# A pre-normed layer of differential attention and a zoned feed-forward: Wb's weighting on ScalarE, lambda's chain ahead of feed-forward, X summed on TensorE

## What is computed

```python
xn = layernorm(x)                                  # without weights
out = x + attention(xn) + feed_forward(xn)

# attention: 16 half heads of 8 features for q and k, 8 heads of 16 for v
q, k, v = xn @ Wq.T, xn @ Wk.T, xn @ Wv.T          # q, k with rotary tables
probs = softmax(q @ k.T)                           # per half head
lam = exp(sum(lq1 * lk1)) - exp(sum(lq2 * lk2)) + LAMBDA_INIT
attn = (probs[even] - lam * probs[odd]) @ v
attn = attn * rsqrt(mean(attn**2) + 1e-5) * (1 - LAMBDA_INIT)
attention = attn @ Wo.T

# feed_forward: a router picks 3 of 8 zones per sequence, with weights w
z = sum over the 3 zones e of w[e] * (gelu(xn @ Wa[e]) @ Wb[e])
feed_forward = xn + z
```

## Time and profile before

| | |
|---|---|
| three runs | 435.41, 437.92, 437.03 us; median 437.03 |
| profiled execution | 436.09 us, its span 433.6 us |
| PE busy | 414.3 us (96%) |
| DVE busy | 384.8 us (89%) |
| ACT busy | 338.5 us (78%) |
| POOL busy | 141.3 us (33%) |
| feed-forward's second halves | from 39.6 us |
| attention's exponentials | from 141.5 us to 418.3 |
| TensorE's granted clock, mean | 0.992 |

### The profile page before, as it was taken

How to read it: one execution, slowest core, us unless ns; L and a number is a source line. 1 busy time by engine, 2 the same in 40 slices (tenths; PEclk the granted TensorE clock), 3 DMA queues, 4 the chain that set the end, 5 groups by cost and what they waited for, 6 DMA issues and landing times.

```text
span 433.6 us, 7697 instructions
## 1 busy us (share of the span) xinstructions
PE 414.3 (96%) x2742; PEld 191.7 (44%) x2742; DVE 384.8 (89%) x743; ACT 338.5 (78%) x450; POOL 141.3 (33%) x172
## 2 busy tenths in 40 slices
PE   8899999999999999999999999999999999999983
PEld 6665556666655333333333333333333333345442
DVE  4995999999998899999999999999999998888476
ACT  3786656655553799899899989989999999889971
POOL 4269999878763500111020110120112201000002
PEclk9999999999998999999999999999999999999998
DMA  9736751400000070020002064000000000000003
GB/s 269 295 87 221 235 210 51 139 9 1 3 0 2 2 245 1 3 97 3 2 2 99 1 130 68 3 2 2 2 4 0 3 0 3 3 2 2 2 2 97
DMA packets 21871, 24.94 MB, mean 58 GB/s; under 512 B 11818, under 2 KB 16106, under 8 KB 21578
## 3 DMA queue, kind: packets, MB, share of 16 engines
q1 hardware_dynamic: 21096, 23.60, 17.8%
q10 hardware_dynamic: 738, 0.86, 0.8%
HBM read 14.49 MB, written 8.65 MB: 53 GB/s over the span
## 4 chain that ended last, share of the span: by engine, by line
PE 71%; DVE 14%; ACT 7%; issue 5%; DMA 1%; POOL 1%; ACTq 0%; POOLq 0%; DVEq 0%
PE ps L1399 21%; PE ps L1362 16%; PE ps L1252 13%; DVE part_max L905 7%; ACT E L795 5%; PE ps L1324 4%; PE ps L1177 3%; PE ps L1179 3%; PE ps L1178 3%; PE ps L1325 2%; PE ps L1326 2%; PE ps L1390 2%; DMA X<-in_x 1%; PE ps L1380 1%; DVE stats L859 1%
## 5 line engine op out<-in xcount | busy, mean ns | idle before, releaser
L905 DVE TENSOR_REDUCE part_max<-ps 128x1 f32<-128x512 f32 x512 | 320.2, 680 | 26.6 <-PE ps L1252 22.4
L795 ACT ACTIVATE E<-ps 128x1024 f32<-128x1024 f32 x256 | 245.3, 1029 | 30.6 <-PE ps L1362 27.2
L1399 PE MATMUL ps<-E,Vg 128*32 128x512 f32 x896 | 119.3, 605 | 0.0
L1252 PE MATMUL ps<-K,Q 32*128 32x512 f32 x384 | 106.9, 466 | 1.1 <-DVE part_max L905 0.4
L1362 PE MATMUL ps<-Q,K 32*128 32x512 f32 x320 | 70.7, 489 | 2.1 <-ACT E L795 1.4
L1362 PEld LDWEIGHTS ps<-Q,K 32*128 32x128 f32 x320 | 28.6, 181 | 82.7 <-ACT E L795 72.3
L559 POOL TENSOR_TENSOR hL<-h,hH 128x512 fp32r<-128x512 f32 x48 | 61.3, 1286 | 11.6 <-ACT hH L763 11.3
L1252 PEld LDWEIGHTS ps<-K,Q 32*128 32x128 f32 x384 | 45.7, 183 | 24.8 <-DVE part_max L905 18.6
L761 ACT ACTIVATE h<-ps 128x512 f32<-128x512 f32 x48 | 28.8, 599 | 32.1 <-PE ps L1179 22.6
L610 POOL TENSOR_TENSOR U<-AT,rsum 128x256 f32<-128x256 f32 x15 | 9.3, 621 | 104.3 <-DVE rsum L1057 104.3
L1252 PE MATMUL ps<-xnL,xnH 32*128 32x512 f32 x128 | 41.9, 453 | 0.9 <-DVE part_max L905 0.7
(11 more groups left out here) (166 smaller groups left out, 405.1 us busy)
## 6 DMA issues: line engine op xcount, KB each, us to landing
K<-k_scr SPq DMA_DIRECT2D x5, 512.0 KB, 3.8
Q<-q_scr SPq DMA_DIRECT2D x5, 512.0 KB, 7.1
tab<-in_tables SPq DMA_DIRECT2D x2, 1024.0 KB, 10.0
wa_raw<-in_wa SPq DMA_DIRECT2D x6, 256.0 KB, 2.7
wb_raw<-in_wb SPq DMA_DIRECT2D x6, 256.0 KB, 2.9
Q<-max_turned SPq DMA_DIRECT2D x80, 2.0 KB
X<-in_x SPq DMA_DIRECT2D x2, 512.0 KB, 7.0
k_scr<-V SPq DMA_DIRECT2D x2, 512.0 KB, 10.9
```

The lines of the kernel that those rows point to most:

```text
L795: nc.scalar.activation(E[:, par, 2 * jj:2 * jj + 2, :].rearrange("p j t -> p (j t)"), ps[:, 2 * jj:2 * jj + 2, :].rearrange("p j t -> p (j ...
L905: nc.vector.tensor_reduce(part_max[:, tile // FC % 2, j * FC + tile % FC, sh:sh + 1], ps[:, SLOT_BANK[x], :], AX.X, ALU.max).then_inc(slot ...
L1252: mm(ps[:, SLOT_BANK[x], :], Qs[g % KQ_BUFS][strip(j), tile % TB * P:(tile % TB + 1) * P], Ks[g % KQ_BUFS][strip(j), sh * BANK:(sh + 1) * ...
L1399: last = mm(ps[QUAD * j:QUAD * (j + 1), B_PV, :], Vg[:, par, st, j // 2, :], E[:, s % 2, k, :], start=(st == 0), stop=(st == TB - 1), skip ...
```

## The change

Three things are changed, on all five queues.

- *Weighting.* `wb_zone` moves from DVE to ACT, where it is two activations with the zone's weight as scale, both from the raw Wb: one into wb_f, one into the high part. It stands behind gelu of a zone's unit 4. POOL's low part waits for both, SP's `raw_next` for the second.
- *Lambda.* The three parts become one, ahead of the loop of units.
- *The end.* In steps 101 to 113 POOL splits X into two fp32r parts, which take the place of xn's parts in xnH and xnL (groups 3 and 4 of K and Q lay there, their scores are done), and makes an identity in fp32r. At the end PE multiplies both parts by the identity into the product's bank, and Wo's product is added on top. So the additions on POOL and DVE are gone, and ACT copies all four banks to the output rows. `shares_ahead` covers two chunks instead of three, chunk 2 goes the way of chunk 3 with its own root on ACT, and DVE's order at the end is another.

```diff
-LAMBDA_AT = (30, 34, 38)
-
-AHEAD = CHUNKS - 1
+AHEAD = CB
+
+X_SPLIT_AT = (101, 105, 109, 113)
...
                 sp.wait_ge(wa_split, e + 1)
                 sp.sem_inc(sp_waited, 1)
-                sp.wait_ge(wb_done, e + 1)
+                sp.wait_ge(wbh_done, e + 1)
                 raw_load(e + 2, zones[e + 2])
...
             for c in range(CHUNKS):
-                if c < CB:
-                    sp.wait_ge(added, c + 1)
-                else:
-                    sp.wait_ge(o_added, c - CB + 1)
+                sp.wait_ge(o_done, c + 1)
...
+            def x_parts(c):
+
+                t = slice(c * BANK, (c + 1) * BANK)
+                if c == 0:
+                    pool.wait_ge(x_done, TILES + CHUNKS)
+                    pool.sem_inc(pool_waited, 1)
+                    pool.wait_ge(st_done[0], 2 * STEPS * KQ_BUFS)
+                    pool.sem_inc(pool_waited, 1)
+                    pool.wait_ge(st_done[1], 2 * STEPS * KQ_BUFS)
+                    nc.gpsimd.tensor_copy(identR[:], ident).then_inc(id_done, 1)
+                nc.gpsimd.tensor_copy(xnH[:, t], chunk_rows(X, c)).then_inc(x_high, 1)
+                pool.wait_ge(x_high, c + 1)
+                nc.gpsimd.tensor_tensor(xnL[:, t], chunk_rows(X, c), xnH[:, t], ALU.subtract).then_inc(x_split, 1)
...
-            def wb_zone_high(e):
-                act.wait_ge(wb_done, e + 1)
-                nc.scalar.activation(wbH[:, e % 2, :], wb_f[:, e % 2, :], ACT.Copy).then_inc(wbh_done, 1)
+            def wb_zone(e):
+
+                par = e % 2
+                act.wait_ge(raw_in[par], 32 * (e // 2 + 1))
+                if e == 0:
+                    act.wait_ge(wbc_done, 1)
+                if e >= 2:
+                    act.wait_ge(hs_free, H_BUFS + UZ * (e - 1))
+                w = wbc[:, e:e + 1]
+                nc.scalar.activation(wb_f[:, par, :], wb_raw[:, par, :], ACT.Identity, scale=w).then_inc(wb_done, 1)
+                nc.scalar.activation(wbH[:, par, :], wb_raw[:, par, :], ACT.Identity, scale=w).then_inc(wbh_done, 1)
...
-                if n % UZ == 5 and n // UZ + 1 < PICKS:
-                    wb_zone_high(n // UZ + 1)
+                if n % UZ == 4 and n // UZ + 1 < PICKS:
+                    wb_zone(n // UZ + 1)
...
-            squares(CHUNKS - 1)
-            for c in range(CB):
+            def product_copy(c):
                 act.wait_ge(o_ps, c + 1)
                 nc.scalar.activation(chunk_rows(RES, c), ps[:, O_BANK[c], :], ACT.Copy).then_inc(o_done, 1)
+
+            roots(AHEAD)
+            squares(CHUNKS - 1)
+            product_copy(0)
             roots(CHUNKS - 1)
+            for c in range(1, CHUNKS):
+                product_copy(c)
...
-                if n % UZ == 2 and n // UZ + 1 < PICKS:
-                    wb_zone(n // UZ + 1)
-                if n in LAMBDA_AT:
-                    lambdas(LAMBDA_AT.index(n))
...
             square_sums(0)
             square_sums(1)
+            quarter_rows(0)
+            shares_ahead()
             square_sums(2)
-            shares_ahead()
-            quarter_rows(0)
             normalise(0)
             turn_rows(0)
             normalise(1)
+            turn_rows(1)
             quarter_rows(1)
-            turn_rows(1)
+            shares(2)
             normalise(2)
+            square_sums(3)
             turn_rows(2)
-            square_sums(3)
             shares(3)
             normalise(3)
             turn_rows(3)
...
+            def residual(c):
+                if c == 0:
+                    pe.wait_ge(id_done, 1)
+                t = slice(c * BANK, (c + 1) * BANK)
+                pe.wait_ge(x_split, c + 1)
+                mm(ps[:, O_BANK[c], :], identR[:], xnH[:, t], start=True, stop=False, skip_group_check=True)
+                mm(ps[:, O_BANK[c], :], identR[:], xnL[:, t], start=False, stop=False, skip_group_check=True)
...
             pe.wait_ge(exp_done, 2 * ALL_STEPS)
             heads_sum(3, range(GB - 1))
+            residual(0)
+            residual(1)
+            heads_sum(3, (GB - 1,))
             product(0)
-            heads_sum(3, (GB - 1,))
             product(1)
+            residual(2)
             product(2)
+            pe.wait_ge(a_out, 2 * GROUPS + 1)
+            residual(3)
             product(3)
```

More of the change, by code:

```diff
@@ L227, in build @@
             ("X", [P, TILES, P], F32), ("cst", [P, C_END], F32), ("wo_in", [P, P], F32),
-            ("grow", [P, TILES], F32), ("XN", [P, TILES, P], F32),
+            ("grow", [P, TILES], F32), ("identR", [P, P], F32R), ("XN", [P, TILES, P], F32),
             ("V", [P, GROUPS * TB * 2 * QUAD], F32),
@@ L300, in build @@
         grow_done, x_done = sem("grow_done"), sem("x_done")
-        zb_done, z_in, added = sem("zb_done"), sem("z_in"), sem("added")
+        zb_done, z_in, id_done, x_high, x_split = (
+            sem("zb_done"), sem("z_in"), sem("id_done"), sem("x_high"), sem("x_split"))
         wh_done, w_split = sem("wh_done"), sem("w_split")
@@ L327, in build @@
             sem("at_done"), sem("rsum_done"), sem("u_free"))
-        heads_ps, sq_done, ss_done, std_done, rcp_done, rms_done, an_done, ant_done, o_ps, o_done, o_added = (
+        heads_ps, sq_done, ss_done, std_done, rcp_done, rms_done, an_done, ant_done, o_ps, o_done = (
             sem("heads_ps"), sem("sq_done"), sem("ss_done"), sem("std_done"), sem("rcp_done"), sem("rms_done"),
-            sem("an_done"), sem("ant_done"), sem("o_ps"), sem("o_done"), sem("o_added"))
+            sem("an_done"), sem("ant_done"), sem("o_ps"), sem("o_done"))
         u_last = sem("u_last")
@@ L528, in wb_zone_low @@
                 par = e % 2
+                pool.wait_ge(wb_done, e + 1)
+                pool.sem_inc(pool_waited, 1)
                 pool.wait_ge(wbh_done, e + 1)
@@ L641, in _ @@
                     sums_add(SUMS_ADD_AT.index(s))
+                if s in X_SPLIT_AT:
+                    x_parts(X_SPLIT_AT.index(s))
                 if s % TB == 3 and s > TB:
                     shares_of_rows(s // TB - 1)
[L645 to L653, removed]
         @block.scalar
@@ L772, in sums_copy @@
                 nc.scalar.activation(zT[:, c * BANK:(c + 1) * BANK], ps[:, c, :], ACT.Copy).then_inc(z_out, 1)
-            wb_zone_high(0)
+            wb_zone(0)
             strip_evacuate(2)
@@ L956, in _ @@
             xn_low(3)
[L958 to L964, removed]
             dve.wait_ge(logit_ps, 1)
@@ L1010, in _ @@
             rotary(4)
-            wb_zone(0)
             reduce_slot(0, 2)
@@ L1014, in _, with lambdas @@
             rotary(5)
-            def lambdas(part):
+            def lambdas():
                 nl, ab, cc, c2, nlc = (lt[:, k:k + 1] for k in range(5))
[L1018 to L1035, removed]
@@ new lines, in lambdas @@
+                dve.wait_ge(lam_exp, 1)
+                link(nc.vector.scalar_tensor_tensor(nl, lam_e[:, 1:2], LAMBDA_INIT, lam_e[:, 0:1],
+                                                    ALU.subtract, ALU.subtract))
+                link(nc.vector.tensor_scalar(ab, nl, -1.0, None, ALU.mult))
+                link(nc.vector.tensor_tensor(ab, ab, nl, ALU.max))
+                link(nc.vector.tensor_scalar(ab, ab, 1.0, None, ALU.add))
+                link(nc.vector.reciprocal(cc, ab))
+                link(nc.vector.tensor_scalar(cc, cc, LAMBDA_RANGE, 1.0, ALU.mult, ALU.min))
@@ new lines, in lambdas @@
+                link(nc.vector.tensor_tensor(c2, cc, cc, ALU.mult))
+                link(nc.vector.tensor_scalar(epsc[:], c2, EPS, SQRT_LEAST, ALU.mult, ALU.max))
+                link(nc.vector.tensor_scalar(limit[:], c2, FLT_MAX, None, ALU.mult))
+                link(nc.vector.tensor_tensor(nlc, nl, cc, ALU.mult))
+                link(nc.vector.tensor_scalar(comb[:], cst[:, C_E0:C_E0 + 2 * QUAD], cc, None, ALU.mult))
+                nc.vector.scalar_tensor_tensor(comb[:], cst[:, C_E1:C_E1 + 2 * QUAD], nlc, comb[:],
+                                               ALU.mult, ALU.add).then_inc(comb_done, 1)
@@ L1037, in _ @@
+            lambdas()
             for n in range(UNITS):
@@ L1102, in shares @@
             def shares(c):
-                dve.wait_ge(std_done, 1)
+                dve.wait_ge(std_done, c - AHEAD + 1)
                 nc.vector.reciprocal(sd[:, c, :], sd[:, c, :]).then_inc(rcp_done, 1)
-                dve.wait_ge(rcp_done, 1)
+                dve.wait_ge(rcp_done, c - AHEAD + 1)
                 nc.vector.scalar_tensor_tensor(sd[:, c, :], ss[:, c, :], limit[:, 0:1], sd[:, c, :],
                                                ALU.is_le, ALU.mult).then_inc(rms_done, 1)
-                dve.wait_ge(rms_done, 2)
+                dve.wait_ge(rms_done, c - AHEAD + 2)
             def normalise(c):
@@ L1147, in _ @@
             turn_rows(3)
-            def residual(c):
-                dve.wait_ge(x_done, TILES + CHUNKS)
-                dve.wait_ge(o_ps, c + 1)
```

(5 more changed lines are left out.)

3 lines of the change are left out of this document (2 added, 1 removed).

## The result

The changed kernel takes 430.57 us in the median of four runs (429.37 to 431.15), the kernel before 436.22 (435.19 to 437.92). The ratio is 0.9883, 95% interval 0.9858 to 0.9909: 5.1 us faster, between 4.0 and 6.2. The forecast was 431.4, 5.5 faster. So the size came out; of the five parts one was off by 0.9 us, and another, the end, by 0.3 the other way.

The account below looks back on a forecast made before the run. It took POOL and PE, with DVE nearly full, to bound feed-forward, and PE and DVE attention. Terms 3.0 + 0 + 0 + 0 + 2.5 = 5.5 us gave 431.4 us, range 429.0 to 434.2.

Parts of the forecast that it names:

- part 3: Start of feed-forward: lambda's twelve operations ahead of the units fit DVE's idle time; 0 us, bounds 0 and +1.
- part 5: End of the kernel: new DVE order and X's additions gone from POOL and DVE; 2.5 us gained, bounds 1.0 and 3.2.
- three for "right": Trace signs named beforehand as confirming, on unit intervals and starts, DVE's return, its idle time and the end's 1.15 us operation.
- the held operation: DVE operation at the end, 1.15 us, said to wait for POOL's additions and fall to 0.3 without them.
- sign for "wrong": Trace signs named beforehand as refuting: PE waiting behind a weighting or before the last product, lambda's operations over 1 us, longer steps.
- Part 1: Feed-forward: Wb's weighting leaves DVE, so PE's late units come back; 3.0 us gained, bounds 1.5 and 3.9.
- zone 1's 0.86: Feed-forward: delay of the interval behind zone 1's weighting, said to be swallowed by full POOL but for about 0.2 us.
- Part 2: Feed-forward: ACT's two activations per zone, 0.63 us each, make the next gelu some 0.35 late but cost nothing.
- the pinned chain of part 1: Feed-forward, early units: POOL's low part, then ACT's gelu, then PE's product; full POOL keeps PE from coming earlier.
- The slower rival: Start: all twelve lambda operations wait out a POOL operation, DVE 10 us late, 441 us; chance 0.03.
- Part 4: Attention steps 101 to 113: X's four copies and four subtractions on mostly idle POOL, about 7.6 us of work, cost 0.
- if that dip goes: Rival: TensorE's clock dip between 120 and 140 us vanishes, up to 1.8 us less; chance 0.12 together with a second dip.

Follow-up runs that it names:

- lam_late: The changed kernel with lambda's twelve operations moved into attention, one a step in steps 60 to 71; ratio to the kernel before 0.9883.
- wb_only: The kernel before with only the weighting of Wb moved to ACT, lambda and the end as before; ratio 0.9982.
- x_only: The kernel before with X in two parts on PE and ACT's copies, but DVE's old order at the end; ratio 0.9995.
- order_only: The kernel before with DVE's new order, shares ahead for two chunks and chunk 2's own root, additions of X as before; ratio 0.9950.
- lam_only: The kernel before with only lambda's twelve operations put in one piece ahead of feed-forward; ratio 0.9973.
- tail_only: The changed kernel with the weighting back on DVE and lambda back in the units, so the changed end alone; ratio to the kernel before 0.9924.
- one_wah: The changed kernel with four of lambda's two-tensor operations reading a scalar operand, and Wa's high parts for zones 1 to 5 on ACT; ratio to before 0.9853.
- changed again: The changed kernel unaltered, run again beside other variants on the same chip; ratio to the kernel before 0.9871.

## Why the prediction was right, and where not

The forecast time was right, and in part by luck: part 3 was 0.9 us too good and part 5 0.3 too bad, so the sum of 5.5 stands beside 4.9 us in the traces' stages. Of the signs that it named, three for "right" came (intervals from unit 12 on at 2.02, no DVE idle before the third square sum, the held operation at 0.25), and three did not: unit 8 was 0.75 later and not unmoved, unit 45 2.0 earlier and not 3, DVE back at 41.66 and not at 39.7. One sign for "wrong" came as well, lambda's operations over 1 us.

**Part 1, the weighting: right.** The sum of 3.0 us was made for a start without loss. lam_late, which has such a start, is 2.95 ahead of before at unit 45. The claim that POOL swallows zone 1's 0.86 but for 0.2 was the risky one; wb_only gives 0.14.

**Part 2, ACT: right.** Each activation takes 0.72, not 0.63. The gelu behind a pair is 0.2 late (77.72, where PE's products had ended at 77.51), and no interval of PE shows it.

**Part 3, lambda in front: this step failed.** The prediction took 0, with bounds 0 and +1, because "the pinned chain of part 1 takes such a delay up without loss by unit 8". DVE's delay itself was in the text (five operations, back at 40 to 41; it was 41.66, 1.92 late). Two things were wrong. Nearly all of it reached PE, 1.75 us at unit 1: the ring gives PE four slots, and it needed two reductions more to issue the six in front of unit 1's second half. And a pin takes up a delay only as far as PE had been ahead of it. By part 1's own sum PE would have been 0.86 ahead; the rest of 1.75, 0.9, stays, near the upper bound. It is there: 17.92 at unit 8 for 17.01 in lam_late, which lacks the delay, 92.76 at unit 45 for 91.83; and the two intervals in which the pin holds PE in lam_late (2.36 and 2.50, units 6 to 8) are 2.02 in the changed kernel. I counted the same 0.86 twice, once as given up to POOL and once as cover for lambda beyond its size. By the rule of the Trainium skill cited there (SBUF — State Buffer, "two separate sides") an operation with two SBUF inputs is blocked until the GpSimd operation that holds the port pair has ended; the trace agrees, the three `tensor_tensor` operations end within 0.01 us of POOL's. I had used that rule for the end and set it aside at the start, for the rows of lambda inside the units (0.16 us at 113.70 and 121.97), which had met POOL idle or in its last tenths. The slower rival, all twelve waiting, did not come: the 128x1 operations with one tensor go through at 0.15 to 0.21.

**Part 4: right.** The steps take the same time to 0.1 us, with X's eight operations on POOL and without.

**Part 5, the end: right to 0.3 us.** 2.8 for 2.5. U of the last quarter came 1.8 us earlier against the last table load (4.61 us behind it before, 2.83 now), not 1.4, in part since shares_ahead with two chunks took 3.4 and not 3.6. The held operation (now L1109) takes 0.25. The share of the lock was over-read: 0.8 us was ascribed to it, but x_only shows that without the new order 0.4 is all that X on PE brings, because ACT's root is late next, and order_only that with it 0.4 is all that the additions cost.

**The clock.** The rival "if that dip goes" came true in the profiled execution: 1.15 us of the 6.0. It belongs to that execution and not to the change: wb_only, lam_only and x_only lack the stretch too, tail_only, order_only, lam_late and one_wah have it. The record can split it off, since it has the span and the mean granted clock of every execution, and these go together. Beside lam_late and "changed again", on one chip, the kernel before took spans of 432.1 to 432.6 us at a mean of 0.996 or 0.997 (five), 433.0 to 434.0 at 0.992 or 0.993 (five) and 435.3 at 0.989 (one). The traces say what the levels are: before's, at 0.992, has one stretch inside its work; wb_only's, at 0.997, has none, and half clock only in the last 3 us. The changed kernel without a stretch took 427.2 to 427.4 (four, at 0.999 or 1.000). So with the clock out of it the change is worth 5.0 us between the medians, and the stages give 2.0 + 0.05 + 2.8 = 4.9.

## What to carry to other kernels

A delay is only absorbed by slack that no other term of the sum has spent: carry the positions of the waiting engine unit by unit, not the savings. Before small DVE operations are moved into idle time, look at what POOL does there, not only at DVE's gap; in these runs two SBUF tensors, or a single one of 64 columns, cost up to a POOL operation each beside a full POOL, while an operation on one column whose second operand is read as a per-partition scalar took 0.21 us. And when an addition leaves the last chain, look for what stands ahead of it in the other engine's queue.

## What was not expected of the hardware

- The wait of DVE for POOL hits a 128x1 operation with two tensors (0.15 alone, up to 1.30 beside POOL) as well as a 64-wide `tensor_scalar` on one tensor (0.25 to 1.23), but no 128x1 `tensor_scalar` (at most 0.22 in all traces) and no reduction from PSUM (at most 0.70).
- The stretches at half clock (1.2 GHz) are each 3.4 us long and sit at a few places: in the last units, where PE waits for DVE's reductions; ahead of feed-forward, at 29 us; once at units 36 to 38; once in the first steps. Of the 14 traces 5 have none, and the same program had one in one execution and none in another. They cost 1.15 us in the last units and 1.5 to 1.6 elsewhere, so the time of one profiled execution is uncertain by that much. What decides whether one comes is open: from 23 us to 28.5 PE was busy 4.96 of 5.5 us in the execution of the changed kernel where the clock fell at 29 us, and 4.85 in the one where it did not.
- "Changed again" spent 13.2 us at its end, 0.7 more than all others of that form, with the same rows up to ACT's last copy: the last store landed later.
